# Two halves of a silu moved ahead of the product with C, in a selective scan on one core

## The reference, cut to what matters

```python
act_mx = jax.nn.silu(mx)                  # mx = x_ssm @ Wx.T + bx
delta = jax.nn.softplus(einsum('bsr,er->bse', dlt, Wdt) + bdt)
dA = jnp.exp(delta[..., None] * A)
dBu = delta[..., None] * Bm[:, :, None, :] * u[..., None]
def step(h, xs):
    dA_t, dBu_t, C_t = xs
    h = dA_t * h + dBu_t
    y = jnp.einsum('ben,bn->be', h, C_t)
    return (h, y)
y1 = act_mx * z1                          # z1, z2: forward and backward scans
y2 = act_mx * z2
out = einsum('bse,de->bsd', y1 + y2, Wf) + bf + skip
return x + gate[:, None, :] * out
```

## Time and profile before

| | us |
|---|---|
| median of 3 runs | 3278.92 |
| lowest and highest | 3277.81, 3281.28 |
| the profiled execution, its own time | 3282.95 |
| its span, from first to last instruction | 3281.1 |
| DVE busy | 3014.0 (92%) |
| PE busy | 2988.6 (91%) |
| POOL busy | 2900.1 (88%) |
| ACT busy | 2679.4 (82%) |

### The profile page before, as it was taken

How to read it: one execution, slowest core, us unless ns; L and a number is a source line. 1 busy time by engine, 2 the same in 40 slices (tenths; PEclk the granted TensorE clock), 3 DMA queues, 4 the chain that set the end, 5 groups by cost and what they waited for, 6 DMA issues and landing times.

```text
span 3281.1 us, 54891 instructions
## 1 busy us (share of the span) xinstructions
PE 2988.6 (91%) x19924; PEld 2373.0 (72%) x19924; DVE 3014.0 (92%) x2006; ACT 2679.4 (82%) x5153; POOL 2900.1 (88%) x1280
## 2 busy tenths in 40 slices
PE   8978999899998999899999999899999999899999
PEld 5756666667767666678877766678778666677789
DVE  2739999999999999999999999999999999999994
ACT  1448999988888999987788999987877999988772
POOL 0428999999999999999999999999998999999993
PEclk9989999999999999999999999999999999999999
DMA  5765334644475333645575434645566333645463
GB/s 223 248 230 187 130 119 135 225 160 156 167 250 198 132 130 127 224 151 157 162 246 186 135 118 137 222 140 165 167 217 209 122 131 130 228 137 165 155 199 111
DMA packets 207053, 560.40 MB, mean 171 GB/s; under 512 B 20200, under 2 KB 66472, under 8 KB 202560
## 3 DMA queue, kind: packets, MB, share of 16 engines
q1 hardware_dynamic: 203424, 538.01, 48.9%
q10 hardware_dynamic: 2208, 10.49, 0.9%
q0 software_dynamic: 1152, 8.39, 0.6%
HBM read 476.19 MB, written 80.63 MB: 170 GB/s over the span
## 4 chain that ended last, share of the span: by engine, by line
PE 50%; ACT 20%; DVE 12%; issue 10%; DVEq 0%; ACTq 0%
PE y L880 14%; PE slot L891 10%; PE mb L851 9%; ACT abuf L1129 8%; PE mb L964 6%; DVE hbuf L1322 6%; ACT slot L1191 3%; DVE hbuf L1331 3%; PE mb L861 3%; PE slot L903 3%; DVE slot L1322 3%; ACT dec L1191 2%; ACT soft L1085 2%; PE mb L922 1%; PE mb L957 1%
## 5 line engine op out<-in xcount | busy, mean ns | idle before, releaser
L1235 POOL TENSOR_TENSOR hbuf<-hbuf,cres 128x1024 f32<-128x1024 f32 x704 | 1664.6, 2378 | 143.4 <-DVE hbuf L1322 143.4
L1230 POOL TENSOR_TENSOR bst<-bst,du 128x1024 f32<-128x1024 f32 x512 | 1221.0, 2385 | 46.3 <-DVE du L1266 46.3
L1322 DVE TENSOR_TENSOR_SCAN hbuf<-dec,slot 128x1024 f32<-128x1024 f32 x512 | 1164.9, 2275 | 39.0 <-PE slot L903 27.1
L880 PE MATMUL y<-ident,hbuf 128*128 128x128 f32 x8192 | 1016.1, 273 | 0.0
L880 PEld LDWEIGHTS y<-ident,hbuf 128*128 128x128 f32 x8192 | 924.5, 141 | 104.5 <-issue 104.0
L1129 ACT ACTIVATE abuf<-dut,bt 128x128 f32<-128x128 f32 x3072 | 964.5, 387 | 0.0
L1322 DVE TENSOR_TENSOR_SCAN slot<-slot,bst 128x1024 f32<-128x1024 f32 x320 | 728.3, 2276 | 23.0 <-ACT slot L1191 22.1
L1191 ACT ACTIVATE slot<-delta,par 128x1024 f32<-128x1024 f32 x512 | 568.2, 1110 | 198.1 <-DVE hbuf L1331 185.1
L1191 ACT ACTIVATE dec<-delta,par 128x1024 f32<-128x1024 f32 x512 | 584.1, 1141 | 115.5 <-DVE hbuf L1322 114.9
L891 PE MATMUL slot<-ident,abuf 128*128 128x128 f32 x3072 | 408.4, 276 | 170.4 <-ACT abuf L1129 161.0
L891 PEld LDWEIGHTS slot<-ident,abuf 128*128 128x128 f32 x3072 | 339.0, 141 | 302.8 <-ACT abuf L1129 243.9
(11 more groups left out here) (156 smaller groups left out, 2363.2 us busy)
## 6 DMA issues: line engine op xcount, KB each, us to landing
bst<-bc_s SPq DMA_DIRECT2D x512, 512.0 KB, 4.0
cres<-bc_s SPq DMA_DIRECT2D x128, 512.0 KB, 6.8
wzs<-wz_s SPq DMA_DIRECT2D x64, 256.0 KB, 4.1
yf_s<-yrd SPq DMA_DIRECT2D x32, 512.0 KB, 5.3
ybuf<-yf_s SPq DMA_DIRECT2D x32, 512.0 KB, 4.9
yg_s<-ybuf SPq DMA_DIRECT2D x31, 512.0 KB, 4.4
si_s<-silu SPq DMA_DIRECT2D x28, 512.0 KB, 6.1
silu<-si_s SPq DMA_DIRECT2D x28, 512.0 KB, 5.4
```

What stands on the lines that cost most here:

```text
L880: last = nc.tensor.matmul(y[:, j * P:(j + 1) * P], hbuf[:, q % HR, j * P:(j + 1) * P], ident[:], start=False, stop=(q % N == N - 1), is_tr ...
L1230: nc.gpsimd.tensor_tensor(bst[:, i % BR, :], bst[:, i % BR, :], du[:, k % 2, :], ALU.mult).then_inc(pool_b, 1)
L1235: nc.gpsimd.tensor_tensor(hbuf[:, q % HR, :], hbuf[:, q % HR, :], cres[:, q % N, :], ALU.mult).then_inc(pool_prod, 1)
L1322: nc.vector.tensor_tensor_scan(h[:, ::step], decays[:, ::step], inflows[:, ::step], 0.0, ALU.mult, ALU.add).then_inc(scanned, 1)
```

## The change

Both calls of `silu_half` move to just behind the scan of their chunk and ahead of its product. Nothing is added or removed, and no wait changes its condition.

```diff
                     nc.vector.tensor_tensor_scan(h[:, ::step], decays[:, ::step], inflows[:, ::step], 0.0,
                                                  ALU.mult, ALU.add).then_inc(scanned, 1)
+                    if c == 15 and has_mx(k):
+                        silu_half(k, 0)
+                    if c == 1 and k > 0 and has_mx(k - 1):
+                        silu_half(k - 1, 1)
                     if c == 1 and k > 0 and projection_of(k - 1) is not None:
                         read_projection(projection_of(k - 1), mb[0])
...
-                    if c == 1 and k > 0:
-                        if has_mx(k - 1):
-                            silu_half(k - 1, 1)
                     if c == 5 and k == NU - 1:
...
-                    if c == 15 and has_mx(k):
-                        silu_half(k, 0)
```

## The result

| | before | after |
|---|---|---|
| median of 6 runs | 3280.10 us | 3292.64 us |
| lowest and highest | 3275.66, 3281.92 | 3290.06, 3296.12 |
| ratio after to before | | 1.0039, 95% interval 1.0027 to 1.0051 |
| the profiled execution | 3282.95 | 3291.40 |
| its span | 3281.1 | 3289.6 |

The account below looks back on a forecast made before the run. It took a unit to be bound by waits going round DVE, ACT and PE, with DVE dense from scan 1 to chunk 5's product. 7.3 + 3.0 + 0 = 10.3 us on 3278.92 gives 3289.2 us, range 3285.2 to 3296.9.

Parts of the forecast that it names:

- The step prices: DVE start to start: scan to waiting product 2.33 or 2.31 us, to a non-reader 2.18, product 1.14, silu 0.66.
- Half 1 at the ordinary seams: Chunk 1, 28 seams: silu waits for ACT's sigmoid, scan 2 comes 0.26 us later, 7.3 us in all.
- The rival of absorption: Slack from chunk 5 to the next seam swallows the 0.26 us: 3280.5 us, no change; chance 0.13.
- Half 1 at the four seams: Chunk 1, seams to units 8, 24, 40, 56: late sigmoid, product now follows silu, 0.76 us each, 3.0 in all.
- Half 0: Chunk 15: scan 0 comes 0.08 us later, hidden by DVE's 0.37 us idle ahead of scan 1; no cost.
- The clock: Longer PE idle time brings more seams at its low clock: nine more add 4.6 us, 3293.8 and up; chance 0.16.
- No gain from either: Silu half 1 ending earlier helps neither PE's delta product, as PE then waits for scan 2, nor SP's store in chunk 5.
- The sum: Ordinary seams 7.3, four seams 3.0, chunk 15 nothing: 10.3 us slower, 3289.2 us on the median.
- the ring: Round of waits from DVE through ACT and PE back to DVE, setting unit length; a delay there comes back whole.

Follow-up runs that it names:

- half1_4: Kernel before, with only half 1 of silu ahead of its product, only at the seams to units 8, 24, 40 and 56: 3284.40 us, +4.2.
- half0_only: Kernel before, with only half 0 of silu (chunk 15) moved ahead of its product: 3279.06 us, -1.2, ratio 0.9997.
- filled_after: Changed kernel, with PE's delta product of half 1 in chunk 3 made three times over at 32 seams: 3286.99 us, +6.4 over the kernel before.
- half1_only: Kernel before, with only half 1 of silu (chunk 1) moved ahead of its product, at all 32 seams: 3295.87 us, +15.6, ratio 1.0044.
- short_moved: Kernel before, with the last two instructions of sigmoid half 1 on 8 columns and silu half 1 moved at 28 ordinary seams: 3274.24 us, -6.3.

## Why the prediction was right

The forecast was 3289.2 us, +10.3 over a median of 3278.9; measured were 3292.64 and +12.5, inside the range and above its middle. Of the 3.4 us between forecast and measurement 1.2 are the kernel before, whose median rose from 3278.92 to 3280.10 with more runs; 2.2 are the change.

- **The step prices** held. Silu to product is 0.66 to 0.67, product to scan 1.13, the wait 0.30 in chunk 1 and 0.21 in chunk 15.
- **Half 1 at the ordinary seams**: 0.26 each, 7.3 in sum; 7.5 with the clock out of it. The delay goes round the unit: in the changed kernel PE still waits 1.43 us for ACT in chunk 8, and ACT 0.72 us for PE in chunk 15, so neither took up the 0.26. The rival of absorption is out: 45.75 to 45.77 us for the unit, at each of the 15 ordinary seams at the full clock.
- **Half 1 at the four seams**: 0.76 each, 3.0 in sum. The traces have 0.76 from silu to scan 2, and +2.7 in half1_4; in the changed kernel's trace 2.4, since the unit at the last of the four, 50.57 us long in the trace of before and so the longest there, was 50.27 in that of after; the three others grew by 0.74 to 1.17.
- **Half 0**: nothing. half0_only shows it. The idle time ahead of scan 1 went from 0.37 to 0.31 with the 0.08 us that it hides.
- **The clock** is the term that was mis-sized. I took it at nothing in the sum and as a rival with nine more slow seams for 4.6 us. Eight more came. They cost less each than the 0.51 of rows 11: the eight together 1.6 us in the pair of profiles (9.1 less 7.5), all thirteen 3.8 us by filled_after's ordinary seams. Many were at the low clock for a part of the product only, from 2.66 us for the 16 matmuls up. This could be read in the trace of before: its five slow seams took 3.21 to 3.63 us, and their units were longer by 0.15 to 0.53, 2.2 us in all and not 2.6. I had named the growth of PE's idle time as 0.26 "at least"; it was 0.61. Silu half 1 ends 0.86 us sooner behind scan 1, so PE's delta product no longer stops in its middle, and PE is done 0.34 us sooner, with scan 2 0.26 later. "No gain from either", I wrote of silu's earlier end. It was a small loss. The counts of slow seams among the 28: none where the gap is filled, none at an idle time of 1.02 us, 4 or 5 at 1.16, 4 at 1.35, 11 to 16 at 1.77. The Trainium skill, "TensorE: Matmul & The Clock Gate", Part 1, has the low level follow on idleness; these counts agree with the direction.
- **The sum** as measured: 7.5 at the ordinary seams, 3.0 at the four others and 1.6 from the clock make 12.1 of the 12.5 us.
- **What stays open.** half1_only has a higher median than the kernel with both halves moved, 15.6 against 12.5 over its own kernel before. The intervals overlap (1.0029 to 1.0059, 1.0027 to 1.0051), and its trace has more slow seams, 16 against 13. Whether half 0 has a part in that was not tried. The filling changes two things at once, PE's idle time and what PE does in it, so the runs don't tell which of them keeps the clock up; and which of the ordinary seams turn slow in a given run was not settled.

## What to carry to other kernels

An instruction put between a producer and the consumer that waits for it gained the gap between them (here 0.15 us) only where its own input was there when the producer ended and no wait for the consumer came back to DVE. Before such a move, compare two distances in the trace: from the producer's start to the end of the new instruction's input (here 2.56 us against the scan's 2.18), and who the next waiter for the consumer is (here ACT's decays, in chunk 9). And where an engine is 99% busy in a unit, ask what its one short idle time waits for: here the work on the ring through ACT and PE was worth 21 us (15.7 at the ordinary seams), and the gap in DVE's own queue 4 in the trace of short_moved.

## What the runs showed of the hardware that I had not expected

More work on PE made the changed kernel faster: about 1.7 us of repeated matmuls in an idle time of 1.77 us took the slow products with the diagonal from 13 to none at 28 seams, and the median from +12.5 to +6.4 us. The same work in the kernel before cost 3.5 us, because at four seams it came late and stood in the way. With an idle time longer by 0.6 us they had gone from 5 to 13. At the lower of the two clock levels the 16 matmuls took up to 3.76 us, against 1.95 to 2.02 at the full one.
